# A window-attention block in fp32r: part of the first MLP layer as 64-row matmuls, two chunks beside one another

## The reference

```python
h = layernorm(x, ln2_w, ln2_b)
h = gelu(h @ mlp_w1 + mlp_b1, approximate=False)   # 192 -> 768
x = x + (h @ mlp_w2 + mlp_b2)                      # 768 -> 192
```

## Time and profile before

| | |
|---|---|
| time, median of 3 runs | 3025.48 us (3024.97 to 3027.86) |
| profiled execution, own time | 3029.68 us |
| its span | 3027.8 us |
| granted TensorE clock over the span | 0.995 |
| one group (from one L646 to the next, at 1518.48 and 1541.62 us) | 23.14 us |
| busy, share of the span | PE 99%, PEld 94%, DVE 78%, ACT 76%, POOL 55% |

### The profile page before, as it was taken

The page is one execution under the profiler, slowest core; times in us unless marked ns, Lnnn a source line. Parts: engine busy times, 40 slices in busy tenths (PEclk is TensorE's granted clock), DMA queues, the critical chain, the costliest instruction groups (busy, mean ns, idle before and its releaser), DMA issues.

```text
span 3027.8 us, 114959 instructions
## 1 busy us (share of the span) xinstructions
PE 2994.0 (99%) x43446; PEld 2832.8 (94%) x43446; DVE 2376.4 (78%) x6418; ACT 2302.3 (76%) x4493; POOL 1672.7 (55%) x1934
## 2 busy tenths in 40 slices
PE   7999999999999999999999999999999999999998
PEld 6999999999999999999999999999999999999997
DVE  5887888788778877887788788878877887788775
ACT  4777777777777777777777777777777777777776
POOL 3555555555555555555555555555555555555553
PEclk8999999999999999999999999999999999999999
DMA  1110001001100100010001000100110010001000
GB/s 47 28 29 25 24 26 29 24 24 27 29 24 24 29 26 24 24 30 26 24 25 30 25 24 26 29 24 24 27 29 24 24 29 26 24 24 30 26 25 18
DMA packets 109326, 79.79 MB, mean 26 GB/s; under 512 B 7294, under 2 KB 108782, under 8 KB 109294
## 3 DMA queue, kind: packets, MB, share of 16 engines
q1 hardware_dynamic: 107682, 77.18, 9.4%
q10 hardware_dynamic: 1612, 2.16, 0.2%
HBM read 40.78 MB, written 38.54 MB: 26 GB/s over the span
## 4 chain that ended last, share of the span: by engine, by line
PE 98%; DVE 1%; ACTq 1%; ACT 0%; issue 0%; POOL 0%; DVEq 0%; POOLq 0%
PE ps L836 36%; PE ps L839 16%; PE ps L913 6%; PE ps L945 5%; PE ps L867 5%; PE ps L918 5%; PE ps L964 5%; PE ps L919 4%; PE ps L914 4%; PE ps L915 4%; PE ps L799 3%; PE ps L807 2%; PE ps L929 2%; PE ps L933 1%; PE ps L809 1%
## 5 line engine op out<-in xcount | busy, mean ns | idle before, releaser
L390 POOL TENSOR_TENSOR gl<-g,gh 128x392 fp32r<-128x392 f32 x768 | 788.4, 1049 | 251.1 <-ACT gh L684 250.3
L836 PE MATMUL ps<-zh,w 128*128 128x392 f32 x3072 | 722.7, 350 | 0.6 <-ACT zh L646 0.6
L836 PEld LDWEIGHTS ps<-zh,w 128*128 128x128 f32 x3072 | 532.8, 188 | 65.3 <-ACT vt L672 39.8
L275 POOL TENSOR_TENSOR prob<-prob,rcp 128x588 f32<-128x588 f32 x128 | 152.6, 1192 | 529.6 <-DVE rcp L575 529.6
L424 DVE BATCH_NORM_STATS2 st<-xin 98x6 f32<-98x192 f32 x512 | 145.9, 348 | 321.8 <-DMA xin<-in_x 321.6
L678 ACT ACTIVATE g<-ps,biasf 128x392 f32<-128x392 f32 x768 | 389.9, 575 | 2.9 <-PE ps L836 2.9
L363 POOL TENSOR_TENSOR xb<-xin,projbv 98x768 f32<-98x768 f32 x128 | 234.8, 1834 | 271.3 <-DVE z L437 265.2
L684 ACT ACTIVATE gh<-g 128x392 fp32r<-128x392 f32 x768 | 364.6, 533 | 0.0
L836 PE MATMUL ps<-zh1c,wqkv 128*128 128x392 f32 x1536 | 360.9, 343 | 2.6 <-DVE zh1c L447 2.6
L696 ACT ACTIVATE yn<-ps,cols 64x392 f32<-64x392 f32 x128 | 74.9, 585 | 281.2 <-PE ps L919 281.2
L913 PE MATMUL ps<-gh,w2h 128*128 128x392 f32 x768 | 287.7, 375 | 0.2 <-ACT pt L761 0.2
(11 more groups left out here) (110 smaller groups left out, 7290.8 us busy)
## 6 DMA issues: line engine op xcount, KB each, us to landing
xin<-in_x SPq DMA_DIRECT2D x128, 147.0 KB
out<-yo SPq DMA_DIRECT2D x128, 147.0 KB
xin<-in_x SPq DMA_DIRECT2D x128, 71.2 KB
out<-yo SPq DMA_DIRECT2D x128, 71.2 KB
xin<-in_x SPq DMA_DIRECT2D x128, 54.8 KB
out<-yo SPq DMA_DIRECT2D x128, 54.8 KB
xin<-in_x SPq DMA_DIRECT2D x128, 18.8 KB
out<-yo SPq DMA_DIRECT2D x128, 18.8 KB
```

The lines of the kernel that those rows point to most:

```text
L390: pool.tensor_tensor(gl[:, m, :], g[:, m, :], gh[:, m, :].bitcast(F32), ALU.subtract)\
L836: last = pe.matmul(dst, cols(w, part), act_, start=(n == 0), stop=(n == 4))
```

## The change

For chunks 0 to 3, pass 4 (narrow pair x low weight, 128 rows) is replaced by a matmul over the 64 rows of the narrow high part alone, so the product low x low is no longer computed for these chunks. Chunks 0 and 2 use partitions 0 to 63, chunks 1 and 3 partitions 64 to 127, and chunks 0, 1 and then 2, 3 are issued one behind the other, so that each pair lies on the two row halves of the array, with different PSUM banks. For that the narrow high part must stand whole on each half: `zh2[0:64, 1, :]` now holds it for all tokens (three ACT copies of 64 x 196 in place of two), a new tile `zx2[64:128]` holds it for the other half (its odd blocks are the second of these copies, its even blocks a new ACT copy `twin_high_parts2`, put between `values` and `exponential(i, 1)`). `zh2[64:128, 1, :]` is now the narrow low part for all tokens. PE waits on `zx2_done`, on a nop, ahead of the four small matmuls. `h_done` is counted up by 2 after each pair. Chunks 4 and 5 keep their five passes of 128 rows.

```diff
             def low_narrow2(grp):
                 for odd in range(2):
-                    hi, lo = slice(64 * odd, 64 * odd + 64), slice(64 - 64 * odd, 128 - 64 * odd)
-                    wait(dve, zh2_done, 3, grp, 2 + odd)
-                    last = dve.tensor_tensor(blocks_of(zh2[lo, 1, :], odd), stacked(ps[hi, T2 + 1, 0:M // 2]),
-                                             blocks_of(zh2[hi, 1, :], odd).bitcast(F32), ALU.subtract)
+                    hi = slice(64 * odd, 64 * odd + 64)
+                    high = zx2[hi, :] if odd else zh2[hi, 1, :]
+                    wait(dve, zh2_done, 4, grp, 4)
+                    last = dve.tensor_tensor(blocks_of(zh2[64:128, 1, :], odd), stacked(ps[hi, T2 + 1, 0:M // 2]),
+                                             blocks_of(high, odd).bitcast(F32), ALU.subtract)
                 last.then_inc(zl2_done, 1)
...
                 for odd in range(2):
                     hi = slice(64 * odd, 64 * odd + 64)
-                    act.activation(blocks_of(zh2[hi, 1, :], odd), stacked(ps[hi, T2 + 1, 0:M // 2]), ACT.Copy)\
-                       .then_inc(zh2_done, 1)
+                    high = zx2[hi, :] if odd else zh2[hi, 1, :]
+                    act.activation(blocks_of(high, odd), stacked(ps[hi, T2 + 1, 0:M // 2]), ACT.Copy).then_inc(zh2_done, 1)
+                act.activation(blocks_of(zh2[0:64, 1, :], 1), stacked(ps[64:128, T2 + 1, 0:M // 2]), ACT.Copy)\
+                   .then_inc(zh2_done, 1)
+
+            def twin_high_parts2(grp):
+                wait(act, zh2_done, 4, grp, 2)
+                act.activation(blocks_of(zx2[64:128, :], 0), blocks_of(zh2[0:64, 1, :], 0).bitcast(F32), ACT.Copy)\
+                   .then_inc(zx2_done, 1)
...
                     exponential(i, 0)
                     values(i)
+                if feeds(i):
+                    twin_high_parts2(prev)
+                if attends(i):
                     exponential(i, 1)
...
                 for m in first:
-                    chunk(m, (3, 4), {3: [(zh2_done, 3, prev, 3), (zl2_done, 2, prev, 2)]}).then_inc(h_done, 1)
+                    chunk(m, (3,), {3: [(zh2_done, 4, prev, 4), (zl2_done, 2, prev, 2)]})
+                wait(pe, zx2_done, 1, prev, 1)
+                pe.nop(nofuse=True)
+                for m in first:
+                    r = slice(64 * (m % 2), 64 * (m % 2) + 64)
+                    last = pe.matmul(ps[:, H[m], 0:M], w1[r, 3, 128 * m:128 * m + 128], (zx2[r, :] if m % 2 else zh2[r, 1, :]),
+                                     start=False, stop=True)
+                    if m % 2:
+                        last.then_inc(h_done, 2)
                 for m in range(len(first), KC):
                     chunk(m, range(5)).then_inc(h_done, 1)
```

More of the change, by code:

```diff
@@ L105, in swin_kernel @@
         zl2 = sb("zl2", [128, M], F32R)
+        zx2 = sb("zx2", [128, M], F32R)
         g = sb("g", [128, KC, M])
@@ L155, in swin_kernel @@
         t1_done, zh1_done, zl1_done = map(sem, ("t1_done", "zh1_done", "zl1_done"))
-        t2_done, zh2_done, zl2_done = map(sem, ("t2_done", "zh2_done", "zl2_done"))
+        t2_done, zh2_done, zl2_done, zx2_done = map(sem, ("t2_done", "zh2_done", "zl2_done", "zx2_done"))
         zpad_done = sem("zpad_done")
@@ L450, in low_wide2 @@
             def low_wide2(grp):
-                wait(dve, zh2_done, 3, grp, 1)
+                wait(dve, zh2_done, 4, grp, 1)
                 dve.tensor_tensor(zl2[:, :], ps[:, T2, 0:M], zh2[:, 0, :].bitcast(F32), ALU.subtract)\
@@ L891, in mlp1 @@
                 first = range(4)
-                wait(pe, zh2_done, 3, prev, 1)
+                wait(pe, zh2_done, 4, prev, 1)
                 for m in first:
```

## The result

| | before | after |
|---|---|---|
| time, median of 11 runs each | 3027.09 us (3024.63 to 3028.81) | 3033.21 us (3031.38 to 3034.24) |
| ratio | | 1.0021, 95% interval 1.0011 to 1.0030 |
| profiled execution, own time and span | 3029.68, 3027.8 | 3033.76, 3032.0 |

The changed kernel is 6 us slower, 0.05 us in each of 127 groups. The forecast was 3029 us on the first three runs of before, +4 us; the bounds for that case reached to +8. In absolute terms 3033.21 lies 0.2 above the upper end of that case (3021 to 3033), since the median of before is 1.6 us higher over 11 runs than over 3.

The account below looks back on a forecast made before the run. PE, busy 99% of the span, was taken to bound the kernel. The steps summed to 0.92 us against 0.89 removed, +0.03 in each of 127 groups, so 3025.5 + 4 = 3029 us, range 3003 to 3048 us.

Parts of the forecast that it names:

- (a): Full array to small tiles, from the last pass-3 matmul's start to the first tile's weight load: 0.27 us.
- (b): First small tile's weights are loaded with nothing to hide them: 0.11 us.
- (c): Second tile of the pair, on the other row half, runs together with the first, 0.01 us apart.
- (d): Second pair follows its halves' first matmuls at one distance, 0.18 us, its load hidden under the running matmul.
- (e): From the fourth tile's matmul start to the load of chunk 4's full weights: 0.24 us, bounds 0.21 and 0.27.
- (f): Chunk 4's full weight load, with nothing to hide it: 0.11 us.
- 0.01 left: At `pt`, with Gelu 0.19 late, 0.01 us remains before PE waits; a further 0.05 would cost 6 us.
- (1): Rival: weight loads are not hidden in tile mode, +0.14 us a group, 3043 us; chance 0.15.
- (2): Rival: the row halves take turns on 64-row F32R matmuls, 0.37 us a group, 3073 us; chance 0.10.
- (3): Rival: shape change costs nothing; 0.35 us saved, 0.28 let through by ACT's idle ahead of `oh`, 2990 us; chance 0.10.
- (4): Rival: one of the two shape changes is cheap, by 0.08 to 0.15 us, about 3011 us; chance 0.10.
- (5): Rival: Gelu, `pt` or twin copy 0.1 us later, PE stands 0.1 a group, about 3041 us; chance 0.10.

Follow-up runs that it names:

- (1): Changed kernel with the new ACT and DVE copies, but PE keeps the four 128-row pass 4 matmuls, without nop or twin wait: 3025.21 us, ratio 0.9999.
- (4): Changed kernel with only chunks 0 and 1 as a 64-row pair; chunks 2 and 3 keep 128-row pass 4: 3051.87 us, ratio 1.0096.
- (5): Changed kernel with its four small matmuls issued twice over: 3075.16 us, ratio 1.0172.
- experiment 3: Changed kernel with all four small matmuls on the upper row half, partitions 0 to 63: 3073.44 us, ratio 1.0160.
- (2): Changed kernel without the nop, the twin wait moved to the second small matmul: 3031.21 us, ratio 1.0016.
- experiments 7 to 10: Against experiment 6, four small matmuls added ahead of pv; the first, 64 x 128 fp32r with 392 tokens: 3054.95 us; the others vary the operands.
- experiment 6: Against the kernel of (1), pass 4 left out for chunks 0 to 3, no small matmuls: 2984.22 us, ratio 0.9872.
- run 8: Small matmuls ahead of pv as 64 rows x 64 columns, fp32r, 392 tokens, pass 4 missing from chunks 0 to 3: 3045.81 us, ratio 1.0065.
- run 9: Small matmuls ahead of pv as 64 rows x 32 columns, fp32r, 392 tokens, pass 4 missing from chunks 0 to 3: 3043.11 us, ratio 1.0059.
- runs 11, 12: Small matmuls ahead of pv as plain fp32, 32 columns, 98 tokens, pass 4 missing: 49 rows 3026.51 us, 64 rows 3026.99 us.
- run 10: Small matmuls ahead of pv as 64 rows x 128 columns, plain fp32, 98 tokens, pass 4 missing from chunks 0 to 3: 3062.44 us, ratio 1.0120.

## Why the prediction was right

**The mechanism.** PE's stream between pass 3 and `pv` sets the time; the two distances saved are eaten by two changes of shape and two bare loads. Shown: the new copies alone cost nothing that can be seen (1), one pair costs 28 us (4), two pairs more cost two distances more (5), and so does laying the four on one half (3).

**Step by step.** (a) 0.27: measured 1525.40 to 1525.66, 0.26, and the nop has no part in it (2). (b) 0.11: measured 0.10. (c) 0.01: measured 0.01, 3 ns in the finer record. (d) 0.18: measured 0.18 behind the first pair's real start (0.29 on record less the bare load), and experiment 3 shows the load hidden on the same half. (e) 0.24, between bounds of 0.21 and 0.27: measured 0.27, the upper bound. This term was mis-sized by 0.03 us a group, 4 us. The lower bound came from `pv`: I took its 96 records for 96 matmuls of 0.08 each on their tile; they are 48 matmuls in two records of 0.04, so behind `pv` too the gap is 0.10 and not 0.05. There was no reason for a middle value. (f) 0.11: measured 0.11 (0.63 for two matmuls, before 0.52 in the steady stream). With (e) alone put right the sum is 0.95 against 0.89, +7.6 us. With every term as measured it is 0.26 + 0.10 + 0.01 + 0.18 + 0.27 + 0.11 = 0.93, +0.04 a group or 5 us: the 0.03 too little in (e) and the 0.02 too much in (a) and (b) partly cancelled, and that the forecast came within 2 us is to that extent luck. Measured were 6.1 us between the medians and 4.2 between the spans of the two profiled executions.

**ACT.** `values` and both exponentials start no later: right. The Gelu is late by 0.12, not 0.19: it starts 0.23 behind `spare` where it was 0.11. The small matmul's record ends at 1525.67 + 0.44 = 1526.11 and ACT starts at 1526.15:

```profile
1525.92 0.20 ACT L765 ACTIVATE spare<-ident 1x1 f32<-1x1 f32 x1
1526.15 2.02 ACT L688 ACTIVATE g<-ps,biasf 128x392 f32<-128x392 f32 x4
```

It answers in 0.04 where I had 0.10. The wait of 0.1 to 0.2 that I announced ahead of the Gelu is no row of the list; only the start times show it. The idle time ahead of `oh` was not used up (38.2 over 127 after, 37.7 before, where I expected 0.09 of 0.30 to remain), and here two things of the prediction were wrong. I had ACT "without a gap" between the Gelus and `oh`, but it follows PE once more in between. In the group of the earlier trace rows the copies end at 1526.77 and `pt` starts at 1526.85, 0.84 behind the first of L945 (1526.01); in the changed kernel it starts at

```profile
1528.96 1.22 ACT L774 ACTIVATE pt<-ps 128x588 f32<-128x588 f32 x2
```

again 0.84 behind the first of L966 (1528.12), whose output it copies. So ACT's delay ends at `pt`, but for the 0.05 by which PE itself is later. And I set that delay against a PE that stood still, though my own sum moved it by 0.03. So the "0.01 left" at `pt` and the 6 us for a further 0.05 did not describe this kernel; nothing stood on the edge.

**The rivals.** (1) is refuted: loads are 0.01 apart and hidden (c, d, experiment 3). (2) is refuted by the pair's starts and by experiment 3, which is what it would have cost: 48 us, worked out 47. (3) and (4): no change between full array and tiles is free here, 0.26 to 0.27 each way in the changed kernel and in experiments 2 to 5; experiments 7 to 10 found the gap also between one tile form and another. The cap I gave to (3), 0.28 at `oh`, is near the measured 0.31, but by luck: what limits there is mostly the Gelu of chunk 3 (experiment 6). The page "TensorEngine Tiling (Array Packing)" of the Trainium skill (Theoretical Speedup, up to 2x for 64 rows) fits the pair alone (one distance for two matmuls), not the block: of the 0.36 that it would save, nothing is left and 0.05 is paid on top. (5): no new wait for an engine appears in the list.

**Open.** Whether fp32r tiles of 64 rows x 32 or 64 columns, four or eight beside one another, would have cheaper bare loads (0.05 for 64 columns by run 8) and so turn the balance is not shown; runs 8 and 9 have only the first 64 or 32 of the outputs. Six chunks in one block would by the fixed price save 0.13 a group on PE, an estimate (three distances, 0.53, less 0.40), but hold the first Gelu back by eight matmuls; that was not run.

## What to carry to other kernels

Count a block of small tiles inside a full-array stream as a fixed price plus its packed streams: here about 0.40 us (twice the 0.09 by which 0.27 exceeds a distance, and twice 0.11 of bare load) against 0.18 us for each matmul that is packed away. Two pairs fell 0.05 short of paying; by the same line, an estimate that no run tests, it pays from three pairs on, and only if nothing waits for the first of them. Put small tiles beside small tiles of the same column width and type, since only there was the join free. And before a stretch is called "PE-bound", leave the work out once: 0.71 us a group removed here gave back 0.31.

## What the runs showed of the hardware that was not expected

- A change of type between tiles of the same column width (fp32r 64 x 32 with 392 tokens, then fp32 49 x 32) has the same gap as a change of shape: 0.27 us from start to load with 0.16 of stream (run 9). With type and column width equal it is gone (runs 11, 12); the token count changed along with the type.
- The gap does not grow with the columns of the tile that is left: 0.27 for 32, 0.27 for 64, 0.26 for 128.
- A plain fp32 matmul leaves two records in the trace (four leave eight in run 10, `pv`'s 48 leave 96), an fp32r matmul one, and so does a transpose of fp32 data (L945); durations per matmul must be read accordingly.
- On one and the same row half, 64-row tiles take their weights under the running matmul: four loads of 0.18 in 0.65 us (experiment 3).
